# A graph layer on one core: four node groups counted instead of three, with fuller gaps, a split table and new span loops

## The reference, cut to what matters

```
x (6250, 256), src and dst (200000,), dst sorted, low nodes far more often than high ones
agg   = segment_sum(x[src], dst, 6250)
h     = relu(agg @ W_rel + b_rel + x @ W_root)            # 6250 x 512
gates = h @ W_ih.T + b_ih + b_hh ; i, f, g, o = split(gates, 4)
y     = sigmoid(o) * tanh(sigmoid(i) * tanh(g)) @ W_fc + b_fc
out   = layernorm(x + y)
```

## Time and profile before

| | us |
|---|---|
| median of 3 runs | 1879.01 (1873.73 to 1880.08) |
| profiled execution, its own time | 1876.59 |
| its span, first to last instruction | 1874.6 |
| PE busy | 1478.7 (79%) |
| POOL busy | 1360.6 (73%) |
| DVE busy | 776.2 (41%) |
| mean granted PE clock | 0.889 |

### The profile page before, as it was taken

One profiled execution on the slowest core, in us unless ns is written; L12 is line 12 of the kernel. 1 busy time (PEld: TensorE's weight loads), 2 busy tenths in 40 slices (PEclk: granted clock), 3 DMA queues, 4 the chain that ended last, 5 costly groups with the idle time before them and its releaser, 6 DMA issues.

```text
span 1874.6 us, 32527 instructions
## 1 busy us (share of the span) xinstructions
PE 1478.7 (79%) x6531; PEld 1182.2 (63%) x6532; DVE 776.2 (41%) x1635; ACT 393.2 (21%) x720; POOL 1360.6 (73%) x2094
## 2 busy tenths in 40 slices
PE   0046576677688878988868999888798999999887
PEld 0023354455577767766656887767576888887766
DVE  8666535455322123454453132444544222333222
ACT  0000011121211022323212122332222122322223
POOL 3866778877777777777777777757776767567770
PEclk9985676788799988988888999899988999999999
DMA  7944555555576766555656776645555766556660
GB/s 248 350 136 126 150 170 150 154 171 153 167 233 206 225 180 180 170 158 172 174 171 194 231 233 187 174 128 163 166 160 158 247 190 197 154 160 178 179 177 17
DMA packets 132286, 334.47 MB, mean 178 GB/s; under 512 B 18527, under 2 KB 63228, under 8 KB 130534
## 3 DMA queue, kind: packets, MB, share of 16 engines
q0 software_dynamic: 81984, 267.98, 49.1%
q10 hardware_dynamic: 46248, 48.38, 8.2%
q1 hardware_dynamic: 3936, 16.62, 2.3%
HBM read 313.70 MB, written 19.20 MB: 178 GB/s over the span
## 4 chain that ended last, share of the span: by engine, by line
POOL 37%; issue 28%; PE 24%; DVE 3%; DVEq 3%; POOLq 2%; DMA 1%; ACT 0%; SPq 0%; ACTq 0%
POOL rows L382 27%; PE ps_blk L516 10%; POOL idx L352 9%; PE ps_agg L455 4%; PE ps_y L524 2%; PE ps_win L443 2%; PE ps_blk L498 2%; PE ps_blk L503 2%; POOL rows L367 1%; POOLq L352 1%; DVEq L872 1%; PE ps_win L430 1%; DVE hot_key L877 1%; PE ps_tr L430 1%; DMA rows<-x_parts,idx 1%
## 5 line engine op out<-in xcount | busy, mean ns | idle before, releaser
L382 POOL DMA_INDIRECT rows<-x_parts,idx x1008 | 1032.6, 1024 | 416.5 <-POOL idx L352 164.3
L455 PE MATMUL ps_agg<-rows,onehot 128*125 x1204 | 379.5, 469 | 231.8 <-SPq L321 112.5
L516 PE MATMUL ps_blk<-cell,wih_sb 128*128 128x250 f32 x2400 | 555.0, 390 | 3.2 <-issue 2.1
L516 PEld LDWEIGHTS ps_blk<-cell,wih_sb 128*128 128x128 f32 x2400 | 470.4, 198 | 74.1 <-issue 11.2
L455 PEld LDWEIGHTS ps_agg<-rows,onehot 128*125 128x125 f32 x1204 | 257.4, 220 | 318.3 <-issue 261.7
L886 DVE SCALAR_TENSOR_TENSOR onehot<-iota_f,tile_first,dst_u 128x500 f32 x301 | 224.0, 746 | 279.5 <-PE ps_agg L455 154.7
L352 POOL COPY idx<-src_sb 128x1 int32 x1040 | 280.8, 270 | 15.7 <-issue 8.8
L643 ACT ACTIVATE cell<-ps_blk,bg_sb 128x250 f32<-128x250 f32 x300 | 140.8, 470 | 565.3 <-PE ps_blk L516 445.4
L872 DVE TENSOR_SCALAR rel<-key,span_key x213 | 52.0, 244 | 290.8 <-issue 196.4
L430 PE MATMUL ps_tr<-hot_key,hot_lo 128*128 x344 | 75.7, 341 | 91.1 <-issue 56.9
L877 DVE TENSOR_TENSOR hot_key<-iota_h,rel 128x980 f16 x213 | 141.0, 662 | 0.1
(11 more groups left out here) (120 smaller groups left out, 830.1 us busy)
## 6 DMA issues: line engine op xcount, KB each, us to landing
hot_key<-in_xb ACTq DMA_DIRECT2D x21, 896.0 KB
rows<-x_parts,idx POOLq DMA_INDIRECT x1008
x_t<-in_xT ACTq DMA_DIRECT2D x25, 250.0 KB
x_n<-in_x ACTq DMA_DIRECT2D x25, 250.0 KB
out<-y ACTq DMA_DIRECT2D x25, 250.0 KB
x_parts<-wih_sb SPq DMA_DIRECT2D x4, 1024.0 KB, 6.9
wih_sb<-in_x ACTq DMA_DIRECT2D x6, 512.0 KB, 8.1
x_parts<-cell SPq DMA_DIRECT2D x2, 1024.0 KB
```

The costliest lines, as they stand in the source:

```text
L382: g.indirect_dma_start(rows_f[:, k * QC + j, :], None, x_parts, bass.IndirectOffsetOnAxis(ap=idx[:, k, j:j + 1], axis=0)).then_inc(landed[ ...
L455: ins = mm(o, onehot[:, hot * QC + j, 0:TN], rows[:, ds(slot + j, 1), :].squeeze(1), start=(first and j == 0), stop=False)
L516: last = mm(o, wih_sb[:, k, col:col + P], h_t[:, k, :], start=(k == 0), stop=(k == KH - 1))
```

## The change

DENSE goes from 3 to 4: group 3 is counted and not gathered, TILES falls from 44 to 42 and SPANS rises from 150 to 200. The gaps hold 3, 3, 3, 3 windows for group 0 and 2, 2, 3, 2 for the others, so that a counted group takes six turns and not seven (group 0: five and not six). The tables are made in two rounds: tiles first (`table_ready`), then the split of pieces 3 to 6, then the spans (`spans_ready`). The span loops run over chunk numbers, with a running place in the ring of pairs in place of a remainder. DVE makes the first three one-hot matrices of tile 0 between the splits of the first gathered steps.

```diff
-DENSE = 3
+DENSE = 4
-FIRST_SLOTS, SLOTS = (2, 2, 2, 2), (2, 1, 2, 1)
+FIRST_SLOTS, SLOTS = (3, 3, 3, 3), (2, 2, 3, 2)
+FIRST_HOTS = 3
-PACK = 1024
+PACK = 2048
...
+        def unpack(engine, regs, at):
+            packed, first, past = regs
+            engine.reg_load(packed, table[0:1, at:at + 1] if isinstance(at, int) else table[0:1, ds(at, 1)])
+            engine.reg_alu(first, packed, PACK, ALU.python_divide)
+            engine.reg_alu(past, first, -PACK, ALU.mult)
+            engine.reg_add(past, past, packed)
+            return engine.snap(first, min_val=0, max_val=CHUNKS - 1), engine.snap(past, min_val=1, max_val=CHUNKS)
+        def next_pair(engine, pair, place, more):
+            engine.reg_add(pair, pair, 1)
+            engine.reg_add(place, place, 1)
+            engine.reg_alu(more, place, PAIRS, ALU.is_lt)
+            engine.reg_alu(place, place, more, ALU.mult)
...
-                        with pe.Fori(0, n) as m:
-                            s = pe.snap(s0 + m, min_val=0, max_val=MAX_PAIRS)
-                            half = pe.snap(s % PAIRS, min_val=0, max_val=PAIRS - 1)
+                        first, past = unpack(pe, pe_regs, at)
+                        with pe.Fori(first, past, QC):
+                            s = pe.snap(pair_0, min_val=0, max_val=MAX_PAIRS)
+                            half = pe.snap(place, min_val=0, max_val=PAIRS - 1)
...
+                            next_pair(pe, pair_0, place, more_places)
...
+            count_below(TILES, 0, (tile_first[0:QP, :], tile_end[0:QP, :]))
...
+            link(v.tensor_scalar(row[:, BAD, 0:1], gap[:, 0:1], 2.0 * FIRST_HOTS, None, ALU.is_lt))
...
+            dve.sem_inc(table_ready, 1)
+            split_pieces(POOL_PIECES, PARTS)
+            count_below(SPANS, 2 * TILES + 1, (span_first[0:QP, :], span_end[0:QP, :]))
+            dve.sem_inc(span_counts, 1)
+            dve.wait_ge(spans_counted, 1)
...
+            link(v.scalar_tensor_tensor(hi, hi, float(QC), lo, ALU.mult, ALU.add))
+            link(v.tensor_scalar(hi, hi, -float(QC - 1), None, ALU.add))
...
-            dve.sem_inc(table_ready, 1)
-            split_pieces(3, PARTS)
+            dve.sem_inc(spans_ready, 1)
...
+            for k in range(RING):
+                split_gathered(k)
+                if k < FIRST_HOTS:
+                    visit(0, dve.snap(0 * group0 + k), dve.snap(0 * group0 + k), k * QC)
```

More of the change, by code:

```diff
@@ L397, in _ @@
             pe.wait_ge(const_made, 11)
-            pe.wait_ge(counts_ready, 1)
-            mm(ps_y[0:1, 0:2 * TILES + 2 * SPANS + 1], ones[0:QP, :], counts, start=True, stop=True).then_inc(counted, 1)
+            pe.wait_ge(tile_counts, 1)
+            mm(ps_y[0:1, 0:2 * TILES + 1], ones[0:QP, :], counts[:, 0:2 * TILES + 1], start=True, stop=True).then_inc(tiles_counted, 1)
+            pe.wait_ge(span_counts, 1)
+            mm(ps_win[0:1, 0:2 * SPANS], ones[0:QP, :], counts[:, 2 * TILES + 1:2 * TILES + 1 + 2 * SPANS], start=True, stop=True).then_inc(spans_counted, 1)
             pe.wait_ge(table_ready, 1)
+            pe.wait_ge(spans_ready, 1)
             step_0 = pe.alloc_register("step_0")
@@ L403, in _ @@
             pair_0 = pe.alloc_register("pair_0")
-            n_span = pe.alloc_register("n_span")
+            pe_regs = [pe.alloc_register(name) for name in ("packed", "first", "past")]
+            place = pe.alloc_register("place")
+            more_places = pe.alloc_register("more_places")
+            pe.reg_mov(place, 0)
             pe.reg_mov(step_0, 0)
@@ L991, in turns @@
                 if count == 1:
-                    turn(n, back=min(i, 2), t=t, parts=u.parts, w=w, wins=u.wins)
+                    turn(n, back=min(i, 2), t=t, parts=u.parts, w=w, wins=u.wins, made=FIRST_HOTS if i == 0 else 0)
                 else:
```

65 lines of the change are left out of this document (28 added, 37 removed).

## The result

The changed kernel takes 1825.75 us (median of 4 runs, 1823.99 to 1830.09) where the kernel before takes 1878.68 (1873.73 to 1880.08): a ratio of 0.9726, with a 95% interval of 0.9701 to 0.9752, so 2.7% faster. The prediction was 1865 us, in a range of 1838 to 1897. The profiled execution took 1824.41 us, its span is 1822.5.

A forecast was written before the change was run, and what follows sets the result against it. POOL's gathers were taken to bound the kernel up to group 0's end, PE after it. Group 0 at 587, three periods of 1158 and a rest of 115.5 gave 1860.5 us of span, scaled to 1865 us, range 1838 to 1897.

The forecast's parts named there:

- What bounds: Whole kernel: POOL's gathers bound up to the end of group 0, PE the counting periods and the rest.
- Group 0: 587: Start to the end of turn 4: group 0 ends at 587 us, range 577 to 600.
- keeps its time: First gap of turn 0: six more pairs and a window cost 11 us, an earlier entry offsets them, step 13 does not move.
- The periods' base: Period 2: 423.6 less 40.7 us for the turn that goes, with 50 us idle for old code in new gaps.
- The saving per stop: Stops between spans in a period's gaps: new code saves 0.4 us at each of 26 stops, 10.4 us.
- The clock: Behind every gap of two or three windows PE's clock falls, adding 6.5 us a period.
- the "quicker" rival: Periods: shorter stops hold the clock in half of the gaps, 45 us come back, 1820 us; chance 0.12 below 1845.
- Slower: Gaps: stops keep their length and PE's clock falls in nearly every gap, 1909 us; chance 0.20.
- Its threshold: The slower rival decides when a stop gets shorter by less than 0.17 us: a 14 us margin over 78 stops.
- POOL's wait for PE over 200 us: Sign of the forecast over the whole kernel: POOL waits more than 200 us for PE.
- Periods of 370 or less: Counting periods: a length of 370 us or less shows the quicker rival, where 375 to 395 was expected.
- The 0.2 us behind each gap: Behind each gap in a period: DVE is earlier and saves 0.2 us, taken as 2 us a period.

The follow-up runs named there:

- e4: The changed kernel with three counted groups and the gaps of before, keeping the new span code, tables and start: 1834.59 us.
- e2: The changed kernel with the old span loop on PE alone: 1902.05 us.
- The doses: The changed kernel with one more table load in PE's unpacking, once per window (1853.93 us) or once per span (1885.67 us).
- e9: The changed kernel with one more table load in PE's unpacking of both spans of each window, 200 loads: 1885.67 us.
- e1: The changed kernel with the old span loops on both PE and DVE; groups, gaps, tables and start stay as changed: 1918.18 us.
- e11: The changed kernel with a turn's nine windows in gaps of 3, 3, 3, 0 in place of 2, 2, 3, 2: 1855.85 us.
- e16: The changed kernel with one more table load in each of the 200 unpackings on DVE: 1833.28 us.
- e8: The changed kernel with one more table load in PE's unpacking of each window's first span, 100 loads: 1853.93 us.
- e7: The changed kernel with PE reading its pair counts from a table of their own, without the unpacking: 1802.95 us.
- e10: The changed kernel with the pair counts of a window's two spans packed into one word, so PE loads once per window: 1784.52 us.
- e3: The changed kernel with the old span loop on DVE alone: 1865.03 us.

## Why the prediction was wrong, point by point

**What bounds.** Right. POOL bounds up to group 0, PE the periods from the second on, and only there is the price of a window paid.

**Group 0: 587, measured 588.5.** Right as a sum, by two errors that cancel. e4 has the new code and start with the gaps of before: its group 0 ends at 705.7 us against 727.9, so code and start bring 22 us, of which the prediction kept 4. The fuller gaps then seem to give 19 of them back: by an estimate 705.7 less 21 steps of 6.5 would be 569. That the sum came out is luck. The rows that were foretold are there: index copies at 31.98 (31), a pair in group 0 some 1.2 us after the last on DVE (1.3), and a longer stop of POOL behind the first gap, now before step 12. Step 13 follows at 159.6 us, against 162.9 (it "keeps its time"):

```profile
152.43 0.97 POOL L400 DMA_INDIRECT rows<-x_parts,idx  x1 [19.43 <-PE ps_agg L476]
```

**The periods' base: right.** 40.7 us for the turn that goes (a turn without windows takes 40.5 in the changed kernel), 50 us idle for old code in the new gaps (48.0 in e2), 396.4 + 2 for period 2 (396.8 in e2). Even the busy times foretold, 348.4 and 340.4, are those of e2 with the old code on PE, 348.8 and 340.5.

**The saving per stop: the term that was mis-sized.** The step "0.4 us for each of the 26 stops" had the right 0.4: the step from span to span went from 2.18 to 1.77 us, and the last stop of a gap from 1.44 to 1.04. But it was counted where the stops are seen. The sequencer gains its 0.4 in every span of the gap, also in those it works off ahead of the array, and the gain adds up to the end of its lead. In a gap of two windows the first stop, 1.16 us in the gap of the earlier trace rows, did not shrink by 0.4: it vanished, in all nine gaps of period 2. The count should have been the 50 spans of a period: 50 x 0.4 = 20 us at most, and 16.6 and 15.3 are what the idle time fell by (e2 against the change); 12.4 were predicted. The doses agree: of 7.5 and 15 us more on the sequencer 5.1 and 10.2 come back as idle time in period 2, 3.8 and 12.3 in period 3.

**The clock: the step that failed.** The prediction let PE's clock fall behind every gap of two and three windows, and added 6.5 us a period for it. I cited the Trainium skill (TensorE: Matmul & The Clock Gate, "HAM oscillation") for it. Its case there is a PE that waits for a DMA between short bursts of matmuls and starts every burst at half rate. With the old code on PE the traces agree: the clock falls behind all 11 such gaps of periods 2 and 3 in e2, and in e9 with its added loads too. With the short code it falls behind five of 11 in period 2 and seven of 11 in period 3: both gaps of three, and three or five of the nine gaps of two. So the stops that are taken away come back a second time as faster matmuls: 14.5 and 10.1 us beside 16.6 and 15.3 (e2 against the change). Which single gap keeps its clock is not explained by its stops: behind one with 1.04 and 1.07 us around the fourth span it is 1.00, behind one with a stop of 1.13 us it is 0.66. Only the number over a period follows the code.

That is the "quicker" rival, "if half of the gaps no longer fall": six of 11 and four of 11 no longer do. I had given it 0.12 on the ground that 3.0 of 4.0 us of idle around a gap would remain; in the gap shown 2.1 remain. That its time, 1820 us, is so near has some luck in it: it took 45 us from the clock alone, where 30 of the 39.5 us are faster matmuls and 9 are idle time.

**Slower.** Refuted: it needed the stops to keep their length. But its mechanism is real, as e1, at 1918 us, shows; 1909 was its price. Its threshold was worked out wrongly: a margin of 14 us over 78 stops is 0.18 us a stop, so the gain would be gone when a stop gets shorter by less than 0.22 us (0.4 less 0.18), not 0.17.

**The waits.** "POOL's wait for PE over 200 us" was too much, 157.6: it was worked out with longer periods. Periods of 370 or less were named as the sign of the quicker rival; two of three are. The 0.2 us behind each gap was taken as 2 us, and 12 gaps make 2.4; it changes nothing.

## What to carry to other kernels

In this kernel a run of short matmul groups (0.5 to 0.8 us on the array, 1.7 on the sequencer) behind a long stretch of matmuls begins with a lead of PE's sequencer over the array, three groups with the short code and two with the old, and then goes at the sequencer's step. Where you see that, sum the sequencer's operations over all groups of the run, compare the sum with the lead and the array's own time, and don't count visible stops: a saving of 0.4 us per group took away whole stops. Where PE is the bound, spread such groups over as many gaps as there are, so that the lead is used in each (e11 lost 30 us without it), and shorten the register code of the engine that sets the step before giving it more of them.

## What the runs showed that I had not expected

A table load on PE's sequencer takes 0.30 us, and 200 of them, on an engine whose array is 83% busy, made the kernel 60 us slower (e9), while the same 200 on DVE's made it 7.5 us slower (e16).

The clock can double the price, but not everywhere. From the change to e8 and e9 PE's idle in period 2 goes from 31.4 to 36.5 and 41.6 us, and the time of the same matmuls from 334.3 to 343.7 and 349.0: more than the idle itself. From the change down to e7 and e10 idle falls to 25.3 and 18.4 us, and the matmuls only to 332.8 and 330.8. The sum of idle time does not decide it: e3 has 40.1 us idle and 337.6 busy. The steep part is where the first stop of the two-window gaps comes back. With that stop gone, a further cut gains its own time and little more.

A stop that the profile puts down to another engine's data can be the sequencer's: a pair that had been ready for 4.5 us was named as its releaser.
